# First batch's score stacks and row maxima into the last expert blocks, tables beside batch 0, layer-0 logits transposed

## The chip, the cores and the metric

The kernel runs on one core of one Trainium2 chip. The metric is device time in microseconds of one execution. The engines are TensorE (PE; its weight loads PEld), VectorE (DVE), ScalarE (ACT), GpSimd (POOL) and SyncE (SP, which here only issues DMAs). Each works through its own instructions in order and waits on semaphores.

## What is computed

Two transformer layers on 4 batches of 512 tokens with 256 channels, in float32. Each layer normalises, and adds an attention branch and a mixture of experts, both computed from the normalised rows. Cut to what matters here:

```python
x = hidden                                   # (4, 512, 256)
xn = layernorm(x)
q, k, v = rope(xn @ Wq.T), rope(xn @ Wk.T), xn @ Wv.T      # 16 heads of 16
attn = softmax(q k^T / 4) v
memory = (elu(k)+1)^T v                      # with its norm term, per head
combined = g * memory_readout(elu(q)+1) + (1-g) * attn
x = x + combined @ Wo.T + top2_experts(xn)   # 8 experts, 176 wide, router logits xn @ gate_w.T
xn = layernorm(x)
x = x + gated_linear_attention(xn, decay) + top2_experts(xn)   # 8 experts, 512 wide
```

## The kernel before

The program has three stages, with a barrier and freed semaphores between them (`end_stage`).

**Front (`layer0_front`).** It normalises, routes and runs layer 0's experts and projections. `front_order` writes the order of all engines by hand; each engine walks through it (`walk`) and takes the steps that it has a part in. First come the `prep` steps of the four batches: moments, normalising and turning, router logits (step 2), top two (step 3), weights (step 4). The logits are made per 128 tokens: 24 matmuls with 128 token columns as weights and 8 experts as moving columns, into psL. Then tokens are ranked by expert and gathered in 39 blocks of 128 rows (BLOCKS). A block is gate, turn_h, down, turn (gather and transpose of a later block); TensorE, ScalarE and VectorE pass it on in a chain, and GpSimd gathers and puts rows by indirect DMA. Between these items stand 39 `light` steps, ten per batch: projections of q and k (0, 2), rotation (1, 3), v (4), splitting into three bf16 parts (2 to 8), features, memory (8, 9), and at step 9 SP stores v, features and parts. They are given out evenly over the first 36 (BLOCKS - 3) blocks.

**Middle (`middle`).** Exact attention of layer 0 per batch and group of four heads, as softmax with row maxima. `qst` and `kst` are stacks of bf16 parts, loaded by `load` in 12 DMAs with one of values (`vst`) per group. `rows` makes scores for the maxima, `reduce` takes them on VectorE, `split_max` makes two bf16 parts, `turn_max` transposes them, and `send_max` on SP brings them through memory into two more rows of `qst`. So a group needs its maxima two groups ahead: before the loop, groups 0 and 1 of batch 0 are done in a prologue (L1654 to L1669 on VectorE, L1881 to L1888 on TensorE). In the loop, a group has four slots (`attend`): scores, exponentials, rows of the group after next, values. Beside batch 0 VectorE merges the expert rows of layer 0 that come back from memory (`merge`, two instructions a slot; four batches in four groups). SP loads these rows (L1210) after the stacks, constants and weights; they lie in `held`, with room for three batches. ScalarE makes tables and high parts of the weights before the loop (L1431 to L1442), GpSimd the low parts and the causal mask of the decays (L1345, L1348). Beside batches 1 to 3 run the projections of layer 1 for the batch before; they need the weights and tables.

**Layer 1 (`layer1_main`).** Its experts, with linear attention as light steps. It reads stacks per chunk, which lie in `held` too.

```python
order += [("turn", 0, 0), ("turn", 1, 0), ("gate", 0, 0), ("turn", 2, 0)]
rest, given, used = lights[1:], 0, 0
for b in range(BLOCKS + 1):
    for kind, n in (("gate", b + 1), ("turn_h", b), ("down", b - 1), ("turn", b + 3)):
```

Of the kernel before, what the change touches and what calls it, by code (L numbers as in the profile page):

```python
# [20 lines left out]
P = 128  # L21
# [193 lines left out]
F0H = F0 // 2  # L215
XSLOTS = 4
# [4 lines left out]
def front_order():  # L221
# [9 lines left out]
    for b in range(BLOCKS + 1):  # L231
        for kind, n in (("gate", b + 1), ("turn_h", b), ("down", b - 1), ("turn", b + 3)):
# [160 lines left out]
def layer0_front(nc, io, scratch, keep):  # L393


    with ExitStack() as ctx:
# [34 lines left out]
        hT = [[sb(f"hT{n}{i}", [F0H, 2, P], F32R) for i in range(2)] for n in range(2)]  # L431
        ymem = sb("y", [P, YSLOTS, D])
# [11 lines left out]

        ident_in, consts_in, x_in = sem("ident_in"), sem("consts_in"), sems("x_in", BATCHES)
# [4 lines left out]
        ones, xT_ps, xhi, xlo, logits_ps = (sem(n) for n in ("ones", "xT_ps", "xhi", "xlo", "logits_ps"))  # L450
# [48 lines left out]
        def _(sp):  # L499
# [44 lines left out]
            def light(n, s):  # L544
                if s == 9:
# [16 lines left out]
            walk({"prep": prep, "split": split, "light": light})  # L562
# [6 lines left out]
        def _(pool):  # L569
# [66 lines left out]

            nc.gpsimd.memset(neghalf[:, :], -0.5).then_inc(neghalf_set, 1)
            ranks.set_ones()
            pool.wait_ge(neghalf_set, 1)
            walk({"prep": prep, "split": split, "invert": invert, "turn": turn, "down": down, "light": light})  # L640

        @block.scalar
        def _(act):
# [95 lines left out]
        def _(dve):  # L739
# [109 lines left out]
            walk({"prep": prep, "rank": rank, "invert": invert, "turn": turn, "gate": gate, "turn_h": turn_h, "light": light})  # L849

        @block.tensor
        def _(pe):
            owner = {}

            def prep(n, s):
# [10 lines left out]
                elif s == 2:  # L866
                    pe.wait_ge(xlo, n + 1)
                    pe.wait_ge(routing.copied, n)
                    if n == 0:
                        pe.wait_ge(w_lo, WV + 1)  # L870
                    for t in range(TILES):
                        c = slice(t * P, (t + 1) * P)
                        mm = three(nc, psL[:, t * E:(t + 1) * E],
                                   [(xT[n][0][:, k, c], xT[n][1][:, k, c], wv[0][:, k, D:D + E], wv[1][:, k, D:D + E])
# [1587 lines left out]
```

## Time and profile before

| what | us |
|---|---|
| median of three runs (1073.11 to 1081.39) | 1075.36 |
| profiled execution, as a whole | 1074.24 |
| its span, first to last instruction | 1072.3 |
| front, to the last put of expert rows | 0 to 267 |
| middle's first instruction | 275.67 |

Times in the rows are microseconds from the start of the span unless marked ns. A timeline row gives start, duration, engine, line and operation, out and in, and how many alike were merged; in square brackets is the idle time of the engine before it and what ended that. L1453 is line 1453 of the kernel.

### The profile page before, as it was taken

The numbers are of one execution on the slowest core, as the hardware profiler recorded it, in microseconds if no ns is written. First come the engines' busy times: TensorE is split into PE (matmuls) and PEld (weight loads), VectorE is DVE, ScalarE is ACT, GpSimd is POOL, SyncE is SP. The second block draws the span as 40 slices with busy tenths as digits, with TensorE's granted clock in tenths as the row PEclk, the third lists the DMA queues.
The fourth block names the chain that finished last, engine by engine and source line by source line (L and its number), as shares of the span: only waits on it lengthen the run. The fifth ranks groups of instructions, "written<-read, shape, count | busy, mean of one in ns | idle before, by whom it ended". The sixth has DMA issues, their size and how long they took to land. (4 is left out here: it accounts for less than half of the span.)

```text
span 1072.3 us, 15783 instructions
## 1 busy us (share of the span) xinstructions
PE 866.9 (81%) x4924; PEld 551.0 (51%) x4924; DVE 586.2 (55%) x1296; ACT 423.6 (40%) x734; POOL 348.6 (33%) x265
## 2 busy tenths in 40 slices
PE   3825888787377889989999888657999999999991
PEld 3714877676011233444444345544666666666660
DVE  5595455453385987657766723393334434444435
ACT  2124564655043554774675574041222222222220
POOL 3175657567330000201110030043334344344321
PEclk9967799899556999999989988687999999999995
DMA  6321425334373222234233014449954533644317
GB/s 218 107 54 54 143 98 168 119 109 163 102 222 102 67 71 60 82 109 145 79 108 128 21 70 137 118 146 295 271 181 106 126 89 99 122 98 99 98 39 240
DMA packets 157346, 130.43 MB, mean 122 GB/s; under 512 B 63916, under 2 KB 138684, under 8 KB 157276
## 3 DMA queue, kind: packets, MB, share of 16 engines
q1 hardware_dynamic: 149788, 109.07, 34.5%
q0 software_dynamic: 7488, 20.46, 6.1%
q8 instruction: 40, 0.66, 0.3%
q14 instruction: 30, 0.25, 0.1%
HBM read 83.47 MB, written 46.01 MB: 121 GB/s over the span
## 5 line engine op out<-in xcount | busy, mean ns | idle before, releaser
L1453 DVE TENSOR_REDUCE b_negmax<-b_psM 128x1 f32<-128x512 f32 x256 | 162.8, 682 | 72.0 <-PE b_psM L1700 69.9
L1363 ACT ACTIVATE b_probs<-b_psE 128x512 f32<-128x512 f32 x256 | 138.8, 595 | 130.9 <-PE b_psE L1718 130.3
L1700 PE MATMUL b_psM<-b_kst,b_qst 96*128 96x512 bf16 x256 | 101.8, 443 | 37.5 <-DMA b_vst<-scratch_v 18.2
L1718 PE MATMUL b_psE<-b_qst,b_kst 98*128 98x512 bf16 x256 | 90.9, 419 | 20.9 <-ACT b_probs L1363 10.2
L2066 POOL DMA_INDIRECT scratch_ys<-d_y,put x39 | 39.6, 1016 | 129.3 <-ACT d_y L2098 127.9
L1718 PEld LDWEIGHTS b_psE<-b_qst,b_kst 98*128 98x128 bf16 x256 | 20.9, 99 | 112.0 <-ACT b_probs L1363 50.0
L2218 PE MATMUL d_psG<-d_w,d_xT 128*128 x156 | 76.6, 614 | 2.0 <-DVE d_xT L2117 1.6
L1727 PE MATMUL b_psV<-b_probs,b_vst 128*32 128x512 f32 x512 | 75.5, 664 | 3.0 <-ACT b_probs L1363 3.0
L1700 PEld LDWEIGHTS b_psM<-b_kst,b_qst 96*128 96x128 bf16 x256 | 24.6, 101 | 98.9 <-DVE b_negmax L1453 68.5
L2243 PE MATMUL d_psY<-d_w,d_hidden 128*128 x312 | 74.9, 383 | 0.0
L2226 PE MATMUL d_psU<-d_w,d_xT 128*128 x156 | 74.5, 600 | 0.0
L1305 POOL TENSOR_TENSOR b_combined<-b_both 128x256 f32<-128x256 f32 x16 | 11.6, 726 | 180.2 <-DVE b_both L1497 180.2
L2127 DVE TENSOR_TENSOR d_probs<-d_ps,decay 128x512 f32<-128x512 f32 x64 | 43.6, 687 | 46.7 <-PE d_ps L2261 46.6
L2072 POOL TENSOR_TENSOR d_rs<-d_ss,d_neghalf 128x16 f32<-128x16 f32 x16 | 46.9, 2929 | 56.8 <-DVE d_ss L2156 56.8
L2243 PEld LDWEIGHTS d_psY<-d_w,d_hidden 128*128 128x128 f32 x312 | 57.6, 190 | 12.9 <-issue 6.8
L2098 ACT ACTIVATE d_y<-d_psY 128x256 f32<-128x256 f32 x39 | 14.9, 383 | 122.1 <-PE d_psY L2243 122.1
L2122 DVE TENSOR_TENSOR d_hidden<-d_hidden,d_psU 128x512 f32<-128x512 f32 x39 | 26.8, 687 | 59.7 <-PE d_psU L2226 59.7
L608 POOL DMA_INDIRECT scratch_ys<-a_y,a_rk_put x39 | 43.2, 1108 | 43.8 <-ACT a_y L686 38.6
L2086 ACT ACTIVATE d_hidden<-d_psG 128x512 f32<-128x512 f32 x39 | 23.3, 597 | 86.0 <-PE d_psG L2218 86.0
L581 POOL DMA_INDIRECT a_xg<-scratch_xn,a_rk_take x39 | 41.3, 1059 | 27.9 <-issue 19.3
L2057 POOL DMA_INDIRECT d_xg<-scratch_xn,take x39 | 38.1, 977 | 21.4 <-issue 11.0
L2218 PEld LDWEIGHTS d_psG<-d_w,d_xT 128*128 128x128 f32 x156 | 27.3, 194 | 23.2 <-issue 23.1
(369 smaller groups left out, 1947.3 us busy)
## 6 DMA issues: line engine op xcount, KB each, us to landing
held<-scratch_parts SPq DMA_DIRECT2D x192, 64.0 KB, 3.1
scratch_parts<-a_part SPq DMA_DIRECT2D x12, 512.0 KB
b_qst<-scratch_parts SPq DMA_DIRECT2D x96, 64.0 KB, 2.2
b_kst<-scratch_parts SPq DMA_DIRECT2D x96, 64.0 KB, 2.2
scratch_parts<-b_part SPq DMA_DIRECT2D x24, 256.0 KB, 3.1
scratch_v<-a_v SPq DMA_DIRECT2D x4, 1024.0 KB, 4.5
b_vst<-scratch_v SPq DMA_DIRECT2D x16, 256.0 KB, 2.9
held<-scratch_ys SPq DMA_DIRECT2D x8, 512.0 KB, 6.8
```

What stands on the lines that cost most here:

```text
L581: nc.gpsimd.indirect_dma_start(xg[s], None, scratch["xn0"].rearrange("b s d -> (b s) d"), bass.IndirectOffsetOnAxis(ap=take[:, b:b + 1], a ...
L608: nc.gpsimd.indirect_dma_start(scratch["ys0"], bass.IndirectOffsetOnAxis(ap=put[:, b:b + 1], axis=0), y[b % YSLOTS], None).then_inc(put_ou ...
L1363: nc.scalar.activation(probs[k % PSLOTS][:, h, :], psE[h % 2][:, :], ACT.Exp, scale=float(HD) ** -0.5).then_inc(scores_used[h % 2], 1)
L1453: nc.vector.tensor_reduce(negmax[i][:, t, h:h + 1], psM[:, h % 2, :], AX_X, ALU.max, negate=True).then_inc(rows_used[h % 2], 1)
L1700: nc.tensor.matmul(psM[:, h % 2, :], qst[g][0:STACK, h, t * P:(t + 1) * P], kst[g][0:STACK, h, :], start=True, stop=True).then_inc(rows_re ...
L1718: nc.tensor.matmul(psE[h % 2][:, :], kst[g][0:STACKM, h, k * P:(k + 1) * P], qst[g][0:STACKM, h, :], start=True, stop=True).then_inc(score ...
L1727: mm = nc.tensor.matmul(psV[VW * h:VW * (h + 1), :], vst[g][:, k, VW * h:VW * (h + 1)], probs[k % PSLOTS][:, h, :], start=k == 0, stop=k = ...
L2072: nc.gpsimd.tensor_tensor(rs[:, :], ss[:, :], neghalf[:, :], ALU.pow).then_inc(rs_done, 1)
L2127: nc.vector.tensor_tensor(probs[g][:, :], (ps1 if g % 2 else ps0)[:, :], decay[:, HG * g:HG * g + HG, :].rearrange("p h c -> p (h c)"), AL ...
L2218: mm = nc.tensor.matmul(psG[:, :], xT[b % 2][:, k, :], weights(b, GATE + k * H1, H1), start=k == 0, stop=k == KT - 1)
L2226: mm = nc.tensor.matmul(psU[:, :], xT[b % 2][:, k, :], weights(b, UP + k * H1, H1), start=k == 0, stop=k == KT - 1)
L2243: mm = nc.tensor.matmul(psY[:, 0:D], hT[b % 2][:, k, :], weights(b, DOWN + k * D, D), start=k == 0, stop=k == HT1 - 1)
```

## The change

- `front_order`: light steps are spread over the first 29 blocks (AHEAD = BLOCKS - 10). Behind the turn item of blocks 29 to 32 stands a step `ones`, and behind each of the 32 items of blocks 30 to 37 a step `maxima`.
- The stacks of batch 0's four groups are loaded in the front, at light step 9 of batch n for group n, once that batch's parts are stored; values of all four after batch 3's. They lie on the memory of xT (stacks) and v32 (values), which now stays allocated through the middle; layer 1's chunks lie there as well, so their early load also waits for the last use of the values. Semaphores for stacks, values and maxima are kept across the stages (`Maxima`).
- A `maxima` step is one row-maximum matmul into psT and one reduction for groups 0 and 1; the splits come after steps 15 and 31, the transposes for group 0 after step 19, and SP sends group 0's maxima at step 20.
- `ones`: GpSimd fills the two rows of ones in `kst`.
- The middle has no prologue on TensorE and VectorE. SP issues identity, constants and weights, then returned rows of batches 0 and 1; batches 2 and 3 follow at slots 4 and 8, in a buffer of its own with room for two.
- ScalarE's tables and weight copies stand beside batch 0: sigmoid and small tables after slot 3, two decays after each of slots 4 to 11, weights after 12, 13 and 14. VectorE's waits for them move to the end of batch 0.
- Layer-0 logits: six matmuls with 8 expert columns as weights and 512 tokens moving, a ScalarE copy of 8x512 (step 2), and four transposes into psL (step 3).

```diff
+AHEAD = BLOCKS - 10
...
-            while given < min(len(rest) * used // (4 * (BLOCKS - 3)), len(rest)):
+            while given < min(len(rest) * used // (4 * AHEAD), len(rest)):
                 order.append(rest[given])
                 given += 1
+            if kind == "turn" and AHEAD <= b < AHEAD + GROUPS:
+                order.append(("ones", b - AHEAD, 0))
+            if 0 <= used - 1 - 4 * (AHEAD + 1) < 2 * 16:
+                order.append(("maxima", used - 1 - 4 * (AHEAD + 1), 0))
...
 # front, SP, light step 9
+                    sp.wait_ge(parts_stored, 48 * n + 48)
+                    sp.wait_ge(v_ps, n + 1)
+                    load_group(sp, scratch, keep, 0, n)
+                    if n == BATCHES - 1:
+                        sp.wait_ge(v_stored, 16 * BATCHES)
+                        sp.wait_ge(memory_ps, BATCHES)
+                        for g in range(GROUPS):
+                            load_values(sp, scratch, keep, 0, g)
+            def maxima(p, _):
+                if p == 20:
+                    sp.wait_ge(first.nmT_copied, 1)
+                    sp.dma_start(scratch["max"], nmT).then_inc(first.max_out, 16)
+                    sp.wait_ge(first.max_out, 16)
+                    sp.dma_start(qst[0][STACK:STACKM, :, :],
+                                 scratch["max"].rearrange("(a h) t -> a h t", a=2)).then_inc(first.max_in[0], 16)
...
 # front, GpSimd
+            def ones_rows(g, _):
+                pool.wait_ge(v_ps, g + 1)
+                pool.wait_ge(part_done[2], 2 * BATCHES)
...
+                nc.gpsimd.memset(kst[g][STACK:STACKM, :, :], 1.0).then_inc(ones_set, 1)
...
 # front, ScalarE, prep
+                elif s == 2:
+                    act.wait_ge(logitsT_ps, n + 1)
+                    act.wait_ge(logits_ps, n)
+                    nc.scalar.activation(logitsT[:, :], psH[0:E, :], ACT.Copy).then_inc(logitsT_done, 1)
...
 # front, VectorE
+            def maxima(p, _):
+                n, t, h = p // 16, p // HG % TILES, p % HG
+                if p == 0:
+                    dve.wait_ge(memory_ps, BATCHES)
+                    nc.vector.tensor_copy(identb, ident[:, :]).then_inc(identb_done, 1)
+                dve.wait_ge(first.rows_ready, p + 1)
+                nc.vector.tensor_reduce(first.negmax[n][:, t, h:h + 1], psT[:, h % 2, :], AX_X, ALU.max,
+                                        negate=True).then_inc(first.rows_used[h % 2], 1)
+                if p % 16 == 15:
+                    first.split_max(dve, n, n, False)
+                if p == 19:
+                    dve.wait_ge(first.nmT_ready, 1)
+                    nc.vector.tensor_copy(nmT, psT[0:2 * HG, 0, 0:SEQ // 2].bitcast(BF16)).then_inc(first.nmT_copied, 1)
...
 # front, TensorE
                     pe.wait_ge(xlo, n + 1)
-                    pe.wait_ge(routing.copied, n)
+                    pe.wait_ge(logitsT_done, n)
...
+                    three(nc, psH[0:E, :], [(wv[0][:, k, D:D + E], wv[1][:, k, D:D + E], xT[n][0][:, k, :], xT[n][1][:, k, :])
+                                            for k in range(KT)]).then_inc(logitsT_ps, 1)
+                elif s == 3:
+                    pe.wait_ge(logitsT_done, n + 1)
+                    pe.wait_ge(routing.copied, n)
                     for t in range(TILES):
...
+                        mm = nc.tensor.transpose(psL[:, t * E:(t + 1) * E], logitsT[:, t * P:(t + 1) * P], ident[0:E, 0:E])
...
+            def maxima(p, _):
+                n, t, h = p // 16, p // HG % TILES, p % HG
+                if p == 0:
+                    pe.wait_ge(memory_copied, KT * BATCHES)
+                if p % 16 == 0:
+                    pe.wait_ge(first.stack_in[n], 16 * GROUP_LOADS)
+                if p == 20:
+                    pe.wait_ge(first.nmT_copied, 1)
+                pe.wait_ge(first.rows_used[h % 2], 2 * (p // HG) + h // 2)
+                nc.tensor.matmul(psT[:, h % 2, :], qst[n][0:STACK, h, t * P:(t + 1) * P], kst[n][0:STACK, h, :],
+                                 start=True, stop=True).then_inc(first.rows_ready, 1)
+                if p == 19:
...
+                    for i in range(TILES):
+                        mm = nc.tensor.transpose(psT[0:2 * HG, 0, i * P // 2:(i + 1) * P // 2].bitcast(BF16),
+                                                 first.nmparts[0][:, i, :, :].rearrange("p a h -> p (a h)"), identb)
...
 # middle, SP
-            load(0, 0)
             sp.dma_start(ident[:, :], io["ident"]).then_inc(ident_in, 16)
-            load(0, 1)
...
-            load(0, 2)
-            send_max(1, 0, 0)
-            load(0, 3)
-            for n in range(BATCHES):
...
+            for n in range(2):
+                load_back(n)
+            def returns(k):
+                n = {4: 2, 8: 3}.get(k)
+                if n is not None:
+                    sp.wait_ge(merged, 2 * n - 2)
+                    load_back(n)
...
 # middle, early loads of layer 1 on SP
                 if alone(n):
+                    sp.wait_ge(probs_used, SLOTS * BATCHES)
...
 # middle, GpSimd
-            for g in range(GROUPS):
-                nc.gpsimd.memset(kst[g][STACK:STACKM, :, :], 1.0).then_inc(ones, 1)
...
 # middle, ScalarE
+            tasks = {3: (tables_small,), 12: (weights_hi(wqk, rqk),), 13: (weights_hi(wkv, rkv),), 14: (weights_hi(wr, rr),)}
+            tasks.update({4 + i: (tables_decay(i),) for i in range(HEADS // 2)})
...
 # middle, VectorE
-            for t in range(TILES):
-                reduce(0, 0, t)
-            split_max(0, 0, reused=False)
-            for t in range(TILES):
-                reduce(1, 1, t)
...
-            split_max(1, 1, reused=False)
...
             def ready():
                 dve.wait_ge(merged, 2 * BATCHES)
+                dve.wait_ge(g_done, 1)
...
+                dve.wait_ge(tables, TABLES)
+                dve.wait_ge(w_lo, 3)
...
 # middle, TensorE
+                        pe.wait_ge(value_in[g], 16 * b + 16)
...
-            for t in range(TILES):
-                rows(0, 0, t, 0, range(HG))
-            pe.wait_ge(identb_done, 1)
-            for t in range(TILES):
-                rows(1, 1, t, 0, range(HG))
-                if t == 0:
-                    turn_max(0, 0)
```

## Rows read from the trace of the kernel before

**Rows 1.** The page: busy time of engines, and the exponentials' group.
```profile
PE 866.9 (81%) x4924; PEld 551.0 (51%) x4924; DVE 586.2 (55%) x1296; ACT 423.6 (40%) x734; POOL 348.6 (33%) x265
...
L1363 ACT ACTIVATE b_probs<-b_psE 128x512 f32<-128x512 f32 x256 | 138.8, 595 | 130.9 <-PE b_psE L1718 130.3
```

**Rows 2.** Timeline from the end of the front to the middle's prologue.
```profile
267.05 0.97 POOL L608 DMA_INDIRECT scratch_ys<-a_y,a_rk_put  x1 [0.67 <-ACT a_y L686]
...
275.67 2.95 SPq L1173 DMA_DIRECT2D b_qst<-scratch_parts  x6
...
284.52 1.04 PE L1700 MATMUL b_psM<-b_kst,b_qst 96*128 96x512 bf16 x2 [18.16 <-DMA b_vst<-scratch_v]
...
285.17 11.04 DVE L1453 TENSOR_REDUCE b_negmax<-b_psM 128x1 f32<-128x512 f32 x16
```

**Rows 3.** Timeline from the prologue's second half to the start of group 1.
```profile
299.67 8.26 DVE L1453 TENSOR_REDUCE b_negmax<-b_psM 128x1 f32<-128x512 f32 x12
...
305.12 2.34 POOL L1345 TENSOR_TENSOR b_wkv<-b_outT,b_wkv 128x1024 fp32r<-128x1024 f32 x1
...
307.42 1.01 PE L1718 MATMUL b_psE<-b_qst,b_kst 98*128 98x512 bf16 x2 [0.22 <-issue]
...
307.67 4.50 POOL L1348 TENSOR_TENSOR decay<-decay,b_causal 128x2048 f32<-128x2048 f32 x1
308.03 4.17 DVE L1461 CAST b_nmparts<-b_negmax 128x16 bf16<-128x16 f32 x1
...
312.06 21.57 SPq L1210 DMA_DIRECT2D held<-scratch_ys  x8
...
319.32 0.88 DVE L1680 SCALAR_TENSOR_TENSOR xacc<-held,wts,xacc 128x256 f32<-128x256 f32 x2 [2.94 <-DMA held<-scratch_ys]
...
339.34 1.03 PE L1718 MATMUL b_psE<-b_qst,b_kst 98*128 98x512 bf16 x2 [6.89 <-DMA b_qst<-scratch_max]
```

**Rows 4.** Timeline of VectorE: ends of groups 1 and 3 of batch 0.
```profile
357.91 0.68 DVE L1483 COPY b_outT<-b_psV 128x512 f32<-128x512 f32 x1
...
387.55 0.68 DVE L1483 COPY b_outT<-b_psV 128x512 f32<-128x512 f32 x1
```

**Rows 5.** Windows in group 1: stretch, length, busy us of engines, PEclk, DMA, GB/s.
```profile
339.00:348.00 9.00, 8.66 (x27) 2.08 (x28) 4.98 (x9) 3.54 (x7) 0.00 (x0) 0.50 0.43 121
348.00:360.00 12.00, 10.59 (x51) 2.61 (x50) 10.89 (x22) 7.25 (x14) 0.00 (x0) 0.98 0.18 59
```

**Rows 6.** Timeline of ScalarE: copies of y that end blocks 0, 9, 27, 34, 36, 38.
```profile
95.58 0.38 ACT L686 ACTIVATE a_y<-a_psY 128x256 f32<-128x256 f32 x1 [0.43 <-PE a_psY L58]
...
140.10 0.38 ACT L686 ACTIVATE a_y<-a_psY 128x256 f32<-128x256 f32 x1 [0.34 <-PE a_psY L58]
...
225.22 0.38 ACT L686 ACTIVATE a_y<-a_psY 128x256 f32<-128x256 f32 x1 [0.34 <-PE a_psY L58]
...
258.91 0.38 ACT L686 ACTIVATE a_y<-a_psY 128x256 f32<-128x256 f32 x1 [0.33 <-PE a_psY L58]
...
262.97 0.38 ACT L686 ACTIVATE a_y<-a_psY 128x256 f32<-128x256 f32 x1 [0.33 <-PE a_psY L58]
...
266.39 0.38 ACT L686 ACTIVATE a_y<-a_psY 128x256 f32<-128x256 f32 x1 [1.25 <-PE a_psY L58]
```

**Rows 7.** VectorE: a reduction (ns min/median/max), and a block's instruction by lines.
```profile
L1453 DVE TENSOR_REDUCE b_negmax<-b_psM x256: 669/680/692, 285.2 to 610.9; 128x1 f32<-128x512 f32 x128
...
L790 DVE TENSOR_TENSOR a_xb<-a_psX,a_xb 128x256 fp32r<-128x256 f32 x13 | 5.5, 422 | 12.2 <-ACT a_xb L666 11.9
```

**Rows 8.** TensorE by lines, 95 to 267 us: busy, mean ns, idle before, releaser.
```profile
L964 PE MATMUL a_psT<-a_ident,a_rot 128*128 128x128 f32 x32 | 7.1, 395 | 17.6 <-DVE a_rot L830 17.6
```

**Rows 9.** Timeline of TensorE: batch 3's logits begin; then projections of 512 columns.
```profile
46.17 0.38 PE L56 MATMUL a_psL<-a_wv,a_xT 128*128 128x8 f32 x1 [2.37 <-DVE a_xT L769]
...
51.31 0.77 PE L56 MATMUL a_psT<-a_xT,a_wqk 128*128 128x512 f32 x1
...
55.62 0.39 PE L58 MATMUL a_psT<-a_xT,a_wqk 128*128 128x512 f32 x1
```

More of the change, by code:

```diff
@@ new lines, in front_order, with load_group @@
+    return order
+GROUP_LOADS = 2 * len(Q_PARTS)
+def load_group(sp, scratch, keep, b, g):
+    for op, dst, order in ((0, keep["qst"], Q_PARTS), (1, keep["kst"], K_PARTS)):
+        for i, part in enumerate(order):
+            row = (g % 2) * HG * HD
+            src = scratch["parts"][b, part, KT * op + g // 2, row:row + HG * HD, :]
+            sp.dma_start(dst[g][i * HD:(i + 1) * HD, :, :],
+                         src.rearrange("(h d) t -> d h t", d=HD)).then_inc(keep["first"].stack_in[g], 16)
@@ L639, in _ @@
             pool.wait_ge(neghalf_set, 1)
-            walk({"prep": prep, "split": split, "invert": invert, "turn": turn, "down": down, "light": light})
+            walk({"prep": prep, "split": split, "invert": invert, "turn": turn, "down": down, "light": light,
+                  "ones": ones_rows})
         @block.scalar
@@ L1429, in silu_v @@
                                      ACT.Silu).then_inc(v_done, 1)
-            act.wait_ge(consts_in, CONSTS)
-            nc.scalar.activation(gates[:, 1, :], gates[:, 1, :], ACT.Sigmoid).then_inc(g_done, 1)
-            for k in range(KT):
-                nc.scalar.activation(qdec[:, k, :], after[:, :], ACT.Exp, scale=ldrows[:, k:k + 1]).then_inc(tables, 1)
-            nc.scalar.activation(kdec[:, :], ldall[:, :], ACT.Exp, scale=before[:, 0:1]).then_inc(tables, 1)
-            nc.scalar.activation(cdec[:, :], ldrows[:, :], ACT.Exp, scale=float(CH)).then_inc(tables, 1)
@@ new lines, in tables_decay, with step, weights_hi @@
+            def tables_decay(i):
+                def step():
+                    for n in range(2 * i, 2 * i + 2):
+                        nc.scalar.activation(decay[:, n, :], rel[:, :], ACT.Exp, scale=ldall[:, n:n + 1]).then_inc(tables, 1)
+                return step
+            def weights_hi(dst, src):
+                def step():
+                    act.wait_ge(weights_in, WEIGHTS)
+                    act.wait_ge(padded, 3)
+                    nc.scalar.activation(dst[0][:, :, :], src[:, :, :], ACT.Copy).then_inc(w_hi, 1)
+                return step
@@ L2360, in two_layers, with early @@
             keep["mem"] = inner.enter_context(nc.sbuf_tensor("mem", [P, BATCHES * KT, MW], F32))
+            def early(name, shape, dt=F32):
+                return inner.enter_context(nc.sbuf_tensor(name, shape, dt))
+            keep["xT"] = [[early(f"xT{n}{i}", [P, KT, SEQ], F32R) for i in range(2)] for n in range(BATCHES)]
+            keep["v32"] = early("v32", [P, TILES, HEADS, VW])
+            keep["first"] = Maxima(nc, early)
+            stacks = [[t[:, :, :].rearrange("p a n -> p (a n)").bitcast(BF16) for t in pair] for pair in keep["xT"]]
+            keep["qst"], keep["kst"] = ([pair[i].rearrange("p (h n) -> p h n", h=HG) for pair in stacks] for i in range(2))
+            values = keep["v32"][:, :, :, :].rearrange("p t h w -> p (t h w)")
+            quarter = TILES * HG * VW
+            keep["vst"] = [values[:, g * quarter:(g + 1) * quarter].rearrange("p (t n) -> p t n", t=TILES) for g in range(GROUPS)]
             layer0_front(nc, io, scratch, keep)
```

169 lines of the change are left out of this document (85 added, 84 removed).

## The prediction, before the result was known

> **What bounds the kernel now.** I read the page first, then the timeline from the last expert block of layer 0 to the end of batch 0 of the middle stage, then the front stage by lines and by the copies that end its blocks. The page says TensorE is busy 81% of the span [rows 1]; the stretch that the change touches does not look like that. The last expert row is put out at 267.05. SP issues the first stack load of the middle at 275.67 (I call this point M), and TensorE gets its first row-maximum matmul at 284.52, after 18.16 us without work [rows 2]. Then VectorE paces a prologue of 32 reductions, 0.69 us each (16 in 11.04 us, 12 in 8.26 us) [rows 2, 3]. The first score comes only at 307.42, M+31.7. Group 0 is disturbed as well: a cast takes 4.17 us beside GpSimd's mask, the first merge waits 2.94 us for the returned expert rows, and group 1 waits 6.89 us for its row maxima, which SP could send only after the eight loads of returned rows that it had been issuing for 21.57 us [rows 3]. Group 1 starts at 339.34, M+63.7. After that two groups take 14.8 us each (outT copied at 357.91 and 387.55 [rows 4]), and there VectorE sets the pace: four reductions of 0.69 and two merges of 0.44 fill 3.6 of a slot's 3.7 us [rows 2, 3]. Batch 0 ends at 387.55, M+111.9.
>
> In the front stage the blocks end with a copy of y: 95.58 for the first, 266.39 for the last [rows 6]. From 258.91 to 262.97 lie two blocks with one light step that is not TensorE's, 2.0 us each, from there to 266.39 two with none, 1.7 each; I use 1.95 for a bare block. Nine blocks that carry one batch's light steps took 44.5 us (95.58 to 140.10), 42.6 (the next eighteen, halved) and 37.75 (225.22 to 262.97), so a batch of light steps adds some 20 to 27 us [rows 6].
>
> **The change part by part.**
>
> *Stacks, values and first maxima gone from the middle.* Twelve loads and one value load per group no longer stand ahead in SP's queue there, nor 32 matmuls on TensorE, 32 reductions and two splits on VectorE. Scores of group 0 can begin at M. The 52 loads move into SP's queue among the blocks, where it has only stores; they share the DMA engines with gathers that run four blocks ahead, and I price them at nothing, 2 us at most. What is late next: the first merge, in slot 0 on VectorE, ahead of the reductions of slot 1, for which TensorE's next row matmuls wait. It needs batch 0's returned rows. SP issues them after the identity, eight constants, the expert index and eight weights: 18 issues of 0.49 us (six in 2.95 us [rows 2]) are 8.8 us. In the profile they took 7.3 us from issue to the merge (312.06 to 319.32 [rows 3]), which I take again: M+16.1. Bounds: M+12, because the last two returned loads, issued by 333.63, and two small transfers behind them were through by 339.34 [rows 3], so that 3 us for two loads are possible; and M+20 if weights and four returned loads hinder each other. The maxima of group 1 go out behind the same loads, by about M+20, hidden behind group 0.
>
> From M+16.1: a merge (0.9), then three slots. TensorE will have idled and starts at 1.2 GHz: in group 1 the granted clock was 0.50 until 348 and 0.98 after it [rows 5], and that group took 18.6 us (339.34 to 357.91) in place of 14.8 [rows 3, 4]. So 11.1 for three slots plus 3.8, group 0 ends at M+31.9. Groups 1 to 3 at 14.8 each: M+76.3.
>
> *Tables, weight copies and mask beside batch 0.* ScalarE's 24 copies and tables lie in its idle time: a slot has four exponentials (256 in 138.8 us [rows 1], so 2.2 us of 3.7), and at most two tables or one copy go beside each; two table reloads round the sigmoid at the end of group 0 I put at 0.5 us, since VectorE and not ScalarE paces the slots (bounds 0 and 3). GpSimd's two subtractions of 2.34 us and the mask of 4.50 us [rows 3] now run beside slots 12 to 15. Before, the cast beside the mask took 4.17 us and ended with it, while reductions kept 0.69 us beside the subtractions [rows 3]. So merges and splits can be held, reductions can't. From their place I take 0.5 + 0.5 + 2.4 = 3.4 us; bounds 0 and 9.2 (all three whole). Batch 0 ends at M+80.2, against M+111.9: a gain of 31.7. With all bounds together it lies between 22 and 43.
>
> The Trainium skill (SBUF — State Buffer, Who interferes with whom) says that a VectorE instruction with two SBUF inputs, as a merge is, is shut out for the whole of a GpSimd instruction that reads SBUF, and that a reduction never is. Taken at its worst that is the 9.2 us, and the forecast below would be 6 us later.
>
> *Later loads of returned rows.* Batches 2 and 3 are loaded from slots 4 and 8, after merges 3 and 7. Behind that wait on SP stand the next stack loads, which have a group of slack. Merge 8 comes some 8 us after its issue, merge 12 about the same: nothing, by the 7.3 us above; a miss would cost up to 3 us each. Layer 1's early chunk loads now wait for the last values too, but SP reaches them after batch 3's attention anyway: nothing.
>
> *Maxima in blocks 30 to 37.* Four matmuls and four reductions per block, one behind each item. VectorE's own work per block is three instructions of at most 0.42 us, a reduction 0.68 [rows 7], 0.69 with its gap: 3 x 0.42 + 4 x 0.69 = 4.0 us per block in place of 1.95, over eight blocks 16.4 us; splits, identity cast, and the turn of the maxima at steps 19 and 20 (TensorE, VectorE and TensorE again in turn) 1.5: 17.9 us. TensorE needs less than a bare block's 1.95 and four times at most 0.39 [rows 9], 3.5 us, so VectorE sets it. Bounds: 14 (3.7 us, where successive instructions overlap by 0.1), and 30.7 with TensorE at half clock: twice 1.95 and four matmuls of 0.43, as two overlapping ones in 1.04 us [rows 2] allow, make 5.6 us per block. Queued behind the waits at steps 0, 16 and 20 is the block pipeline of TensorE, but the stacks were loaded long before. GpSimd's four fills of ones stand before puts with three buffers, and SP's waits for stored parts hold only loads that nobody needs yet: nothing.
>
> *Light steps in 29 blocks in place of 36.* The work is the same and blocks are only rearranged, but ten pairs of light steps share a block where there were three. TensorE already stands idle 17.6 us before the key turns, waiting for VectorE's features [rows 8]; with a bare block missing between two dependent steps, up to 1.95 us more can show. Nine new pairs are 17.6 us at most, zero at least. The three pairs of before sit in batches 1, 2 and 3, which were no slower than batch 0 without one (42.6, 42.6, 37.75 against 44.5 [rows 6]), so I lean to the low end: 6 us.
>
> *Logits transposed.* 24 matmuls took 5.14 us per batch (46.17 to 51.31); six of 512 columns cost 0.39 each (51.31 to 55.62 for eleven [rows 9]), 2.4 us, then a copy (0.6, by the 512-column exponentials' 595 ns [rows 1]), four transposes at the old logits' 0.21 each, 0.9, and handovers of 0.3: 4.2 us. But these transposes now stand behind the next batch's token transposes. Over four batches I take 2 us of gain, bounds 4 gained and 1 lost.
>
> **Sum.** -31.7 + 17.9 + 6 - 2 = -9.8 us. The profiled execution took 1074.24, of which 1072.3 is its span, so 1064.4; the median of the runs lies 1.1 above that execution: 1065.5. One per cent, about what a measurement of this kernel can tell from no change, is 10.75 us: below 1064.6 is faster, above 1086.1 slower. The forecast lies almost on the line.
>
> **Rivals.**
> *TensorE falls to 1.2 GHz in blocks 30 to 37.* It then waits for VectorE after every item, and all blocks pay 5.6 us in place of 4.0: 30.7 in place of 17.9, 1078.3, slower than before. It decides from a granted clock near 0.5 over most of these blocks; the break-even is 5.2 us per block. For it: the clock did fall in the middle where TensorE waited [rows 5]. Against it: TensorE would be busy four fifths of each block. The Trainium skill (TensorE: Matmul & The Clock Gate, A second HAM failure mode: psum-queue depth-cycling) tells of such a loss where TensorE idles briefly and often between groups of matmuls that cycle through PSUM banks, as these do; no row here shows it at that load.
>
> *Every pair of light steps costs a whole block.* 17.6 in place of 6: 1077, no change. For it: the idle time in [rows 8] is all chain. Against it: the earlier pairs cost nothing visible.
>
> *The returned rows don't hold.* They land near M+12, and pairs cost nothing: 4.1 + 6 less, 1055.4. For it: the last loads in [rows 3] were that fast. Against it: four loads and the weights go out together.
>
> *The change doesn't start group 0 earlier*, because group 0 only waits elsewhere: that is in the forecast with 16 of 31.7 us; it would have to wait to M+26 to undo the gain.
>
> **How the numbers follow.** Forecast 0.50 (its own range 1057 to 1073), half of it on either side of the line. Half clock 0.16, pairs 0.12, no hold 0.20, something unseen 0.02. Faster: 0.25 + 0.20 = 0.45. Slower: 0.05 of the half-clock case, with late merges and a full 9.2 us, and the unseen: 0.07. The rest, 0.48, is no change. The range reaches to the cases on both sides: 1050 to 1081.
>
> **What would show it.** First score within 2 us of the middle's first SP issue. First merge waiting for the returned rows to about M+16. Group 0's outT near M+32, then 14.8 us per group; one or two merges or casts of 2 us or more near slots 13 to 15. Y copies in blocks 30 to 37 about 4.0 us apart with the granted clock near 1.0. The light blocks over about 6 us later than bare reckoning gives; the middle starting 20 to 24 us later than 275.67. The prediction is wrong if the middle starts before 288 or after 305, or if batch 0 ends before M+70 or after M+90.

## The result, and the profile after

The change makes the kernel slower by half a per cent: median 1083.56 us over 20 runs against 1078.35 over 20 runs of the kernel before, made beside them, a ratio of 1.0052 (95% interval 1.0035 to 1.0069). I had forecast 1065.5 in a range of 1050 to 1081. The profiled execution took 1084.24 us, its span 1082.5. It lies 0.7 us above its median and the profiled one of before 4.1 below its own, so the two profiles are 10.0 us apart where the medians are 5.2. TensorE is as busy as before [rows 1]:

The page of the changed kernel, busy time of engines.
```profile
PE 866.4 (80%) x4868; PEld 546.1 (50%) x4868; DVE 584.5 (54%) x1297; ACT 427.8 (40%) x739; POOL 344.7 (32%) x265
```

The timeline around the start of the middle, answering to [rows 2, 3]:
```profile
293.48 0.97 POOL L679 DMA_INDIRECT scratch_ys<-a_y,a_rk_put  x1 [0.96 <-ACT a_y L769]
...
302.13 0.37 SPq L1302 DMA_DIRECT2D ident<-in_ident_dram  x1
302.31 1.01 PE L1825 MATMUL b_psE<-xT 98*128 98x512 bf16 x2 [9.52 <-PEq L72]
...
311.59 2.24 SPq L1288 DMA_DIRECT2D b_returned<-scratch_ys  x4
...
318.66 0.88 DVE L1781 SCALAR_TENSOR_TENSOR xacc<-b_returned,wts,xacc 128x256 f32<-128x256 f32 x2 [9.89 <-DMA b_returned<-scratch_ys]
...
329.88 1.28 ACT L1542 ACT_TABLE_LOAD   x1
...
331.40 1.28 ACT L1544 ACT_TABLE_LOAD   x1
331.50 0.68 DVE L1599 COPY b_outT<-b_psV 128x512 f32<-128x512 f32 x1
...
334.22 0.92 PE L1825 MATMUL b_psE<-xT 98*128 98x512 bf16 x2 [2.18 <-ACT b_probs L1472]
```

The middle (M, first issue on SP) starts at 302.13, 26.5 us later than before. The prologue is gone: the first score comes 0.2 us behind M, where it came 31.7 behind. The first merge waits for the returned rows to M+16.5. Batch 0 ends at 386.77 (below), M+84.6 against M+111.9 [rows 2, 4]: 27.2 us won, 26.5 paid in the front.

The copies of y that end blocks 0, 29, 37 and 38, answering to [rows 6]:
```profile
101.79 0.36 ACT L769 ACTIVATE a_y<-a_psY 128x256 f32<-128x256 f32 x1
...
256.29 0.38 ACT L769 ACTIVATE a_y<-a_psY 128x256 f32<-128x256 f32 x1 [0.55 <-PE a_psY L58]
...
290.90 0.38 ACT L769 ACTIVATE a_y<-a_psY 128x256 f32<-128x256 f32 x1 [0.33 <-PE a_psY L58]
292.82 0.38 ACT L769 ACTIVATE a_y<-a_psY 128x256 f32<-128x256 f32 x1 [1.54 <-PE a_psY L58]
```

Windows of groups 0 to 3 of batch 0 and of group 0 of batch 1, between the copies of outT (columns as in [rows 5]):
```profile
302.13:331.50 29.37, 19.09 (x71) 4.22 (x72) 14.01 (x29) 11.56 (x20) 1.24 (x4) 0.67 0.44 130
331.50:350.96 19.46, 16.23 (x70) 3.84 (x69) 14.36 (x29) 12.86 (x30) 0.00 (x0) 0.82 0.43 137
350.96:365.79 14.83, 13.37 (x70) 3.42 (x69) 14.19 (x30) 10.68 (x25) 0.00 (x0) 1.00 0.47 143
365.79:386.77 20.98, 14.60 (x68) 3.28 (x67) 20.61 (x30) 10.58 (x19) 9.53 (x4) 0.90 0.17 52
386.77:412.19 25.42, 24.14 (x122) 11.35 (x120) 16.52 (x33) 11.69 (x21) 2.86 (x4) 0.81 0.16 48
```

Three groups are longer than 14.8 us (batch 1's groups do more: its group 0 took 22.1 before). Group 1 begins with TensorE waiting 2.18 us behind two table loads on ScalarE (above); the granted clock, 1.00 from 325 to 333, is 0.50 from 335 to 341, which is 1.2 GHz. In group 3 the merges stand beside GpSimd:

Timeline of group 3, GpSimd, merges and TensorE's wait.
```profile
368.97 2.38 POOL L1454 TENSOR_TENSOR b_wqk<-b_rqk,b_wqk 128x1024 fp32r<-128x1024 f32 x1 [65.55 <-ACT b_wqk L1558]
...
369.31 2.72 DVE L1781 SCALAR_TENSOR_TENSOR xacc<-b_returned,wts,xacc 128x256 f32<-128x256 f32 x2
...
372.87 2.38 POOL L1454 TENSOR_TENSOR b_wkv<-b_rkv,b_wkv 128x1024 fp32r<-128x1024 f32 x1 [1.52 <-ACT b_wkv L1558]
...
374.35 1.58 DVE L1781 SCALAR_TENSOR_TENSOR xacc<-b_returned,wts,xacc 128x256 f32<-128x256 f32 x2
...
377.76 4.52 POOL L1457 TENSOR_TENSOR decay<-decay,b_causal 128x2048 f32<-128x2048 f32 x1
...
378.25 4.72 DVE L1781 SCALAR_TENSOR_TENSOR xacc<-b_returned,wts,xacc 128x256 f32<-128x256 f32 x2
...
383.62 1.21 PE L1806 MATMUL b_psM<-xT 96*128 96x512 bf16 x2 [3.32 <-DVE negmax L1579]
```

Each of the three pairs of merges ends 0.68 or 0.69 us after the GpSimd instruction (371.35, 375.25, 382.28), in place of 0.87 us after its own start: 1.85 + 0.71 + 3.85 = 6.4 us. Behind the last, TensorE has idled 3.32 us and its two matmuls take 1.21 us in place of 0.60; the next group has a granted clock of 0.81 (0.50 from 383 to 396) and takes 25.42 us in place of 22.09.

The table gives these stretches for all kernels run, in us: from the first gather to the last y, blocks 30 to 37 (between the copies of y of blocks 29 and 37; before and in logits_alone light steps stand in six of them), groups 0 to 3 of batch 0 from M, group 0 of batch 1, and from there to the end of batch 3's third group. The names of the experiments are those used below.

| kernel | gather to y | blocks 30-37 | g0 | g1 | g2 | g3 | b1 g0 | rest |
|---|---|---|---|---|---|---|---|---|
| before | 182.6 | 30.1 | 57.2 | 25.0 | 14.8 | 14.8 | 22.1 | 224.0 |
| changed | 208.3 | 34.6 | 29.4 | 19.5 | 14.8 | 21.0 | 25.4 | 230.3 |
| after_again | 209.9 | 34.5 | 29.7 | 19.6 | 14.8 | 21.0 | 26.9 | 227.0 |
| mask_pieces | 209.9 | 34.6 | 29.4 | 19.5 | 14.8 | 16.9 | 21.1 | 227.0 |
| sigmoid_early | 209.7 | 34.5 | 29.5 | 14.8 | 14.8 | 22.3 | 27.0 | 227.0 |
| returned_first | 210.0 | 34.7 | 19.1 | 19.5 | 14.8 | 21.0 | 25.4 | 230.3 |
| all_three | 210.2 | 34.6 | 22.9 | 14.8 | 14.8 | 16.9 | 21.1 | 224.0 |
| lights29 | 192.7 | 17.6 | 54.0 | 22.9 | 14.8 | 14.8 | 22.1 | 224.2 |
| logits_alone | 184.4 | 32.5 | 56.2 | 24.3 | 14.8 | 14.8 | 22.1 | 227.1 |
| maxima_narrow | 202.9 | 27.9 | 29.3 | 19.3 | 14.8 | 22.4 | 22.5 | 225.3 |
| steps_narrow | 202.4 | 27.3 | 30.1 | 18.0 | 14.8 | 22.3 | 25.7 | 226.0 |
| exp_gate | 209.6 | 34.6 | 19.1 | 15.0 | 14.8 | 16.9 | 21.1 | 226.6 |
| exp_gate_old_logits | 210.5 | 34.0 | 19.2 | 14.8 | 14.8 | 16.9 | 21.1 | 227.2 |

### The profile page after: what moved, and what is told of

Its sections match the earlier page's. It is cut to its first block and busy times, and to the rows that moved or that the text cites. A ratio compares the mean times of both kernels' runs of the same rounds, so it can differ in the third digit from the quotient of the medians.

```text
span 1082.5 us, 15716 instructions
## 1 busy us (share of the span) xinstructions
PE 866.4 (80%) x4868; PEld 546.1 (50%) x4868; DVE 584.5 (54%) x1297; ACT 427.8 (40%) x739; POOL 344.7 (32%) x265
## 5 line engine op out<-in xcount | busy, mean ns | idle before, releaser
L1579 DVE TENSOR_REDUCE negmax<-b_psM 128x1 f32<-128x512 f32 x224 | 142.0, 681 | 75.0 <-PE b_psM L1806 74.5
L1825 PE MATMUL b_psE<-xT 98*128 98x512 bf16 x256 | 90.9, 419 | 25.0 <-ACT b_probs L1472 12.1
L1806 PE MATMUL b_psM<-xT 96*128 96x512 bf16 x224 | 83.2, 421 | 26.0 <-DVE negmax L1579 22.8
L1825 PEld LDWEIGHTS b_psE<-xT 98*128 98x128 bf16 x256 | 21.0, 100 | 120.2 <-issue 62.0
L1835 PE MATMUL b_psV<-b_probs,v 128*32 128x512 f32 x512 | 78.6, 689 | 1.8 <-ACT b_probs L1472 1.8
L1806 PEld LDWEIGHTS b_psM<-xT 96*128 96x128 bf16 x224 | 21.2, 101 | 69.9 <-DVE negmax L1579 59.0
L879 DVE TENSOR_TENSOR a_h<-a_h,a_psG 128x176 f32<-128x176 f32 x39 | 13.1, 335 | 52.3 <-ACT a_h L756 52.3
```

Source lines behind the costliest of these rows:

```text
L1579: nc.vector.tensor_reduce(negmax[i][:, t, h:h + 1], psM[:, h % 2, :], AX_X, ALU.max, negate=True).then_inc(rows_used[h % 2], 1)
L1806: nc.tensor.matmul(psM[:, h % 2, :], qst[g][0:STACK, h, t * P:(t + 1) * P], kst[g][0:STACK, h, :], start=True, stop=True).then_inc(rows_re ...
L1825: nc.tensor.matmul(psE[h % 2][:, :], kst[g][0:STACKM, h, k * P:(k + 1) * P], qst[g][0:STACKM, h, :], start=True, stop=True).then_inc(score ...
L1835: mm = nc.tensor.matmul(psV[VW * h:VW * (h + 1), :], vst[g][:, k, VW * h:VW * (h + 1)], probs[k % PSLOTS][:, h, :], start=k == 0, stop=k = ...
```

## The experiments

### The changed kernel again (after_again)

> The changed kernel once more. Theory A (the slower groups of batches 1 to 3 follow from the change): the first group of batch 1 takes 25.4 us again where it took 22.1 before, and the other groups lose the same 6 us as in the first profile. Theory B (the clock falls at points that vary between executions): group 3 of batch 0 is again 21.0, but the later groups differ from the first profile by one to three us, up or down, with the granted clock. Time 1.005 of before by both.

1085.31 us (ratio to before 1.008, 1.0049 to 1.0112). Group 3 is 20.98 again, and group 0 of batch 1 is slow again, 26.9: that far theory A holds, though the size varies: in the kernels below that keep GpSimd's long instructions this group took 22.5 to 27.0 (22.5 in maxima_narrow, where the clock fell to 0.53 inside group 3 already). Behind it theory B does. The rest took 227.0, 3.3 less than in the first profile. The kernel logits_alone (below), whose middle is that of before, shows a step of the same size in code that nothing was done to.

### GpSimd's mask and subtractions in pieces (mask_pieces)

```diff
-            nc.gpsimd.tensor_tensor(decay[:, :, :], decay[:, :, :], causal[:, :].unsqueeze(1).to_broadcast((P, HEADS, CH)),
-                                    ALU.mult).then_inc(masked, 1)
+            for n in range(HEADS):
+                nc.gpsimd.tensor_tensor(decay[:, n, :], decay[:, n, :], causal[:, :], ALU.mult).then_inc(masked, 1)
```
and the subtractions of wqk and wkv in four column ranges each.

> GpSimd's mask in 16 instructions and its two large subtractions in 4 each, in the same places, with the same elements. Theory A (a merge is held until the GpSimd instruction that runs has ended): a merge is held by some 0.6 us at most, group 3 of batch 0 takes 15 to 16.5 us in place of 21.0, TensorE does not fall to 1.2 GHz there, the first group of batch 1 comes back from 25.4 to about 22, and the time falls by 6 to 9 us. Theory B (the two engines share the way to the memory, for so many elements): the pairs of merges lose the same 6.4 us in smaller portions, group 3 stays at 20 to 21, the time the same.

1074.42 us, 10.9 less than the changed kernel in the same comparison (some 7 by the ratio of 1.0052 in the result above), and level with before (0.9985, 0.9965 to 1.0005). Theory A, with group 3 at 16.9 a little above its range. Group 3, GpSimd and merges:
```profile
371.10 3.16 POOL L1456 TENSOR_TENSOR b_wqk<-b_rqk,b_wqk 128x256 fp32r<-128x256 f32 x4 [65.56 <-ACT b_wqk L1562]
371.44 1.55 DVE L1785 SCALAR_TENSOR_TENSOR xacc<-b_returned,wts,xacc 128x256 f32<-128x256 f32 x2
...
378.72 6.57 POOL L1462 TENSOR_TENSOR decay<-decay,b_causal 128x128 f32<-128x128 f32 x14
379.20 1.27 DVE L1785 SCALAR_TENSOR_TENSOR xacc<-b_returned,wts,xacc 128x256 f32<-128x256 f32 x2
```
Its windows, group 3 and group 0 of batch 1:
```profile
367.91:384.83 16.92, 14.15 (x71) 3.44 (x69) 16.78 (x29) 11.89 (x21) 12.69 (x22) 1.00 0.23 69
384.83:405.90 21.07, 19.23 (x118) 9.46 (x118) 16.59 (x35) 10.38 (x20) 4.15 (x8) 1.00 0.18 54
```
GpSimd now works longer (12.69 us in place of 9.53 in the group), but a pair of merges is held for 0.4 to 0.7 us. Against after_again, group 3 is 4.1 us shorter and the group behind it 5.8: the merges are held for less time, and TensorE keeps its full clock in both groups.

### Sigmoid earlier (sigmoid_early)

```diff
-            tasks = {3: (tables_small,), ...
+            tasks = {0: (tables_small,), ...
```

> Sigmoid and small tables after slot 0 in place of slot 3, while VectorE waits for the returned rows. Theory A (group 1 took 19.5 us because the two table loads stop TensorE at the group's start and leave it at 1.2 GHz): group 0 stays at 29 to 30 us, group 1 takes 15 to 16, the time falls by 3.5 to 5 us. Theory B (the clock falls there anyway, after the half-idle group 0): group 1 takes 17.5 to 19.5, the time falls by 2 or less.

1082.04 us, 3.3 less than the changed kernel. The intervals of the two overlap (1.0035 to 1.0073 of before here, 1.0049 to 1.0112 there), so the time by itself shows no gain. The trace does; the window of group 1:
```profile
333.39:348.21 14.82, 13.36 (x70) 3.40 (x69) 14.18 (x29) 10.66 (x25) 0.00 (x0) 1.00 0.59 179
```
Group 1 takes 14.82 us in place of 19.5, at a granted clock of 1.00: theory A. A part comes back later: group 3 takes 22.3 in place of 21.0.

### Returned rows of batch 0 first (returned_first)

```diff
             sp.dma_start(ident[:, :], io["ident"]).then_inc(ident_in, 16)
+            load_back(0)
...
-            for n in range(2):
-                load_back(n)
+            load_back(1)
```

> Returned rows of batch 0 loaded right behind the identity, ahead of constants and weights. Theory A (the first merge waits for nothing but its own rows): it comes 6 to 8 us after the middle's first SP issue in place of 16.5, group 0 ends 8 to 10 us earlier, and the time falls by 7 to 10 us. Theory B (the loads of weights and constants, or the maxima of group 1 that are sent behind them, then end last): the merge comes earlier, but group 1 waits at its start, and the time falls by 3 or less.

1074.51 us, 10.8 less (0.9983 of before, 0.9962 to 1.0003). The issue and the first merge, with the first scores of group 1:
```profile
304.25 0.37 SPq L1302 DMA_DIRECT2D ident<-in_ident_dram  x1
...
304.67 0.97 SPq L1288 DMA_DIRECT2D b_returned<-scratch_ys  x2
...
310.95 0.88 DVE L1781 SCALAR_TENSOR_TENSOR xacc<-b_returned,wts,xacc 128x256 f32<-128x256 f32 x2
...
324.58 0.61 PE L1825 MATMUL b_psE<-xT 98*128 98x512 bf16 x2 [1.67 <-DMA xT<-scratch_max]
```
The merge comes at M+6.7 and has no wait before it any more; group 0 takes 19.1 us in place of 29.7, a little more than theory A's 8 to 10. The wait of theory B is there, 1.67 us at the start of group 1, but that group takes 19.5 us with it as without.

### All three (all_three)

> The three edits together (mask and subtractions in pieces, sigmoid after slot 0, returned rows of batch 0 first). If the three losses are separate, batch 0 of the middle takes 84.6 less 5, 4 and 8, about 67 to 69 us from its first SP issue, the first group of batch 1 some 22, and the time is 18 to 22 us under the changed kernel, 1.2 to 1.6% under the kernel before. If they hide each other (the slots are then paced by VectorE at 1.2 GHz of TensorE), it is 8 to 14 under the changed kernel, at most 0.8% under the kernel before.

1064.10 us, 0.9865 of before (0.9836 to 0.9895); in the comparison with after_again the changed kernel stood at 1.008. Batch 0 takes 69.5 us from M. The three losses are separate (67 to 69 us were expected of batch 0), but for one thing: group 0 takes 22.9 us where it took 19.1 with the returned rows alone. The sigmoid now waits for its input in the first slots, and TensorE for the exponentials behind it:
```profile
314.59 0.22 ACT L1546 ACTIVATE b_gates<-b_gates 128x16 f32<-128x16 f32 x1 [2.66 <-DMA b_gates<-in_gate_attn_dram]
314.83 1.28 ACT L1548 ACT_TABLE_LOAD   x1
...
317.64 0.91 PE L1829 MATMUL b_psE<-xT 98*128 98x512 bf16 x2 [2.58 <-ACT b_probs L1476]
```

### Light steps in 29 blocks, alone (lights29)

```diff
-            while given < min(len(rest) * used // (4 * (BLOCKS - 3)), len(rest)):
+            while given < min(len(rest) * used // (4 * (BLOCKS - 10)), len(rest)):
```
This is the kernel before, with its own middle.

> The kernel before with one edit: light steps over 29 blocks in place of 36. Theory A (pairs of light steps in a block cost a part of a bare block): the last y copy comes 4 to 9 us later, the middle is the same, the time grows by 4 to 9 us. Theory B (the front only shifts the work): within 2 us.

1083.26 us, 1.0062 of before (1.0041 to 1.0084): by itself this one line loses as much as the whole change. The last copy of y comes 9.0 us later (275.34 against 266.39): theory A. From first gather to last y the edit adds 10.1 us (192.65 against 182.55), because the first gather, ahead of which nothing was edited, came 1.15 earlier. In its profile the middle is not the same as theory A has it: groups 0 and 1 with the prologue are 5.3 us shorter than before (77.0 against 82.2), and SP issued the eight loads of returned rows there in 18.17 us in place of 21.57; why was not taken apart. The stretch to 0.4 us behind the last y in both kernels, first before, then lights29:
```profile
83.84:266.77 182.93, 146.06 (x900) 134.35 (x900) 91.00 (x189) 101.59 (x205) 118.70 (x95) 0.88 0.37 124
```
```profile
82.69:275.72 193.03, 149.02 (x900) 136.51 (x900) 89.73 (x189) 101.64 (x205) 115.26 (x95) 0.87 0.35 118
```
The same 900 matmuls; TensorE idles 44.0 us in place of 36.9, and is busy 3 us longer. The bare blocks behind the light ones give a better price than I had (copies of y of blocks 29, 37, 38):
```profile
256.15 0.38 ACT L686 ACTIVATE a_y<-a_psY 128x256 f32<-128x256 f32 x1 [0.33 <-PE a_psY L58]
...
273.71 0.38 ACT L686 ACTIVATE a_y<-a_psY 128x256 f32<-128x256 f32 x1 [0.56 <-PE a_psY L58]
275.34 0.38 ACT L686 ACTIVATE a_y<-a_psY 128x256 f32<-128x256 f32 x1 [1.25 <-PE a_psY L58]
```
Eight take 17.56 us, 2.2 each, not 1.95. The maxima in the same blocks therefore add 34.6 - 17.6 = 17.0 us.

### Transposed logits, alone (logits_alone)

The kernel before with the hunks of the change that concern `logitsT` (front, TensorE and ScalarE, prep steps 2 and 3).

> The kernel before with the transposed logits alone. Theory A (what I forecast: 6 matmuls of 512 columns and 4 transposes for 24 matmuls): the first gather comes 1 to 3 us earlier. Theory B (the handovers over ScalarE eat the gain, as the profile of the changed kernel shows): the first gather comes 0 to 1 us later, and the time is the same within 1.5 us.

The first gather comes at 84.10 in place of 83.84: theory B, nothing is won. Nor can a loss be told: the first gather came between 82.7 and 85.3 in the three profiles with the old logits (before, lights29, exp_gate_old_logits), between 84.1 and 86.6 with the new. The time, 1.0022 (0.9999 to 1.0046), does not separate a small loss from none. The trace shows where the gain went: VectorE's low part of batch 3's rows (L769, L775) and its copy of batch 3's logits (L166), in the kernel before and then in this one:
```profile
44.90 1.22 DVE L769 TENSOR_TENSOR a_xT<-a_psG,a_xT 128x1024 fp32r<-128x1024 f32 x1 [0.93 <-ACT a_xT L652]
...
51.49 0.19 DVE L166 COPY a_rt_logits<-a_psL 128x32 f32<-128x32 f32 x1 [3.70 <-PE a_psL L58]
```
```profile
46.61 1.22 DVE L775 TENSOR_TENSOR a_xT<-a_psG,a_xT 128x1024 fp32r<-128x1024 f32 x1
...
51.74 0.19 DVE L166 COPY a_rt_logits<-a_psL 128x32 f32<-128x32 f32 x1 [3.36 <-PE a_psL L883]
```
Batch 3's logits take 1.5 us less, from their first matmul (46.17 before, 47.88 here) to the copy, but they begin 1.7 us later. Batch 2's logits, which now pass through ScalarE and are turned behind batch 3's token transposes, reach VectorE at 43.41 in place of 42.01, and VectorE takes batch 2's top two ahead of batch 3's low part. From 40 to 52 us TensorE was busy 6.8 us in place of 9.6, at a granted clock of 0.53 in place of 1.00. The profile also shows why a difference of 3 us in the time need not be the logits': group 3 of batch 1, where nothing was edited, in the kernel before and then in this one:
```profile
452.39:479.67 27.28, 25.11 (x136) 12.60 (x134) 15.27 (x30) 22.45 (x28) 2.13 (x1) 0.94 0.34 110
```
```profile
453.45:482.96 29.51, 26.97 (x137) 14.64 (x137) 15.27 (x30) 23.01 (x29) 2.15 (x1) 0.88 0.32 104
```
VectorE's busy time is the same to a hundredth; the granted clock is not.

### Narrow reductions, then narrow steps (maxima_narrow, steps_narrow)

```diff
-                nc.vector.tensor_reduce(first.negmax[n][:, t, h:h + 1], psT[:, h % 2, :], AX_X, ALU.max,
+                nc.vector.tensor_reduce(first.negmax[n][:, t, h:h + 1], psT[:, h % 2, 0:P], AX_X, ALU.max,
```

> The changed kernel with each of the 32 reductions in the blocks over 128 keys in place of 512 (so the maxima of groups 0 and 1 of batch 0 are over a quarter of the keys). A reduction falls from 0.68 to some 0.2 us. Theory A (VectorE's busy time paces blocks 30 to 37): 32 x 0.45, the eight blocks take some 14 us less, 18 in place of 32.4. Theory B (the chain TensorE, ScalarE, VectorE and back paces them, with a reduction in the way of each step and the matmuls added): 5 to 9 us less, 23 to 27.

The second kernel has the matmul over 128 keys as well:
```diff
-                nc.tensor.matmul(psT[:, h % 2, :], qst[n][0:STACK, h, t * P:(t + 1) * P], kst[n][0:STACK, h, :],
+                nc.tensor.matmul(psT[:, h % 2, 0:P], qst[n][0:STACK, h, t * P:(t + 1) * P], kst[n][0:STACK, h, 0:P],
```

> As the kernel with narrow reductions, and the 32 matmuls of the maxima are over 128 keys too. There the eight blocks took 27.9 us, against 34.5 with full reductions and 17.6 where no maxima stand in them. Theory A (the rest of 10.3 us is TensorE's time for 32 matmuls of 512 columns): a matmul falls by some 0.16 us, the blocks take 22 to 24 us. Theory B (the rest is the two handovers that each step puts into the chain): 26 to 28 us.

Reduction and matmul in blocks 30 to 37 of the changed kernel, the reduction of maxima_narrow, then both of steps_narrow (lines: busy us, mean ns, idle before):
```profile
L938 DVE TENSOR_REDUCE negmax<-a_psT 128x1 f32<-128x512 f32 x32 | 21.0, 679 | 0.3 <-PE a_psT L1096 0.3
...
L1096 PE MATMUL a_psT<-xT 96*128 96x512 bf16 x30 | 12.1, 404 | 2.8 <-DVE negmax L938 2.7
```
```profile
L938 DVE TENSOR_REDUCE negmax<-a_psT 128x1 f32<-128x128 f32 x31 | 8.8, 284 | 1.1
```
```profile
L938 DVE TENSOR_REDUCE negmax<-a_psT 128x1 f32<-128x128 f32 x31 | 8.0, 280 | 0.3
...
L1096 PE MATMUL a_psT<-xT 96*128 96x128 bf16 x30 | 6.8, 227 | 0.7 <-DVE negmax L938 0.6
```
The reductions' busy time falls by 12 us, the eight blocks by 6.6 (34.5 to 27.9; the 32.4 of the expectation was a shorter stretch). A matmul falls from 404 to 227 ns, and the blocks by only 0.6 more, to 27.3. So of the 17 us that the maxima cost, some 7 go with the width and 10 remain with quarter-wide steps, 0.3 us a step on average: theory B twice, by the time won. Of what the rest consists was not taken apart. The times are 1078.21 us for maxima_narrow (0.9999 of before, 0.9979 to 1.0018) and 1072.99 for steps_narrow (0.9969, 0.9948 to 0.9991).

Not all of the 7 us is width. The windows of the eight blocks in the changed kernel, of the one among them in which the maxima of group 0 are turned, and a VectorE line over the eight blocks:
```profile
256.67:291.28 34.61, 28.12 (x152) 20.22 (x150) 26.37 (x57) 10.66 (x30) 18.76 (x16) 0.95 0.33 103
274.37:281.14 6.77, 5.56 (x27) 4.03 (x25) 4.40 (x10) 1.47 (x5) 0.97 (x1) 0.75 0.07 22
```
```profile
L879 DVE TENSOR_TENSOR a_h<-a_h,a_psG 128x176 f32<-128x176 f32 x7 | 2.4, 337 | 7.5 <-ACT a_h L756 7.5
```
That block takes 6.77 us where the blocks ahead of it take some 4.4, at a granted clock of 0.75 (0.50 from 278 to 280); in both narrow kernels the clock is 1.00 throughout. This block and the next give 2.3 of the 6.6 us that maxima_narrow wins. VectorE is busy 26.4 of the 34.6 us and waits 7.5 for ScalarE's step behind the gate matmuls, so its sum alone does not pace the blocks at full width either.

### A version that beats both (exp_gate, exp_gate_old_logits)

All three edits, with the tables back behind slot 3 and the sigmoid as 1/(1+exp(-x)), which needs no other table:
```diff
-                nc.scalar.activation(gates[:, 1, :], gates[:, 1, :], ACT.Sigmoid).then_inc(g_done, 1)
+                nc.scalar.activation(gates[:, 1, :], gates[:, 1, :], ACT.Exp, scale=-1.0).then_inc(g_done, 1)
...
+                nc.vector.tensor_scalar(gates[:, 1, :], gates[:, 1, :], 1.0, None, ALU.add).then_inc(omg_done, 1)
+                dve.wait_ge(omg_done, 1)
+                nc.vector.reciprocal(gates[:, 1, :], gates[:, 1, :]).then_inc(omg_done, 1)
```

> As all three edits together, but the gate is made after slot 3 from an exponential on ScalarE and a reciprocal on VectorE, so no other table is loaded beside batch 0. Theory A (the 22.9 us of group 0 there, against 19.1 with the returned rows alone, are the table loads of slot 0): group 0 takes 19 to 20 us, groups 1 and 2 14.8 each, and the time is 3 to 5 us under that of all three, 1059 to 1061, 1.6% under the kernel before. Theory B (group 1 starts at 1.2 GHz whatever ScalarE does): group 0 19, group 1 18 to 19, the time that of all three.

> The same with the logits as in the kernel before. Theory A (the transposed logits cost something, 2.9 us with an interval from 0 to 5 where they stood alone): 1 to 4 us less than with them. Theory B (they cost nothing and that difference came from where the clock fell): the same within 1.5 us.

The second kernel also undoes the hunks of `logitsT`. exp_gate: 1060.86 us, 0.9846 of before (0.9818 to 0.9874). Groups 0 and 1 take 19.1 and 15.0: theory A for the groups; the time's interval overlaps that of all_three. With the old logits 1059.81, 0.9828 (0.9800 to 0.9856); the intervals overlap, so the logits stay open, and cost at most little. Batch 0 of the middle is now 65.8 us (303.73 to 369.58 in exp_gate), against 111.9 before.

## Why the prediction was wrong

The picture was right and the sum was not. The first score at M and the first merge at M+16.5 (forecast M+16.1) came as written, and no marker that I had set for "wrong" was passed (middle between 288 and 305, batch 0 ending between M+70 and M+90). Other signs failed: the middle began 26.5 us later and not 20 to 24, groups 1 and 3 took more than 14.8, and blocks 30 to 37 came 4.4 us apart, once 6.8, and not 4.0. Several terms were off, and all but the maxima against the forecast.

| term | forecast | measured | from |
|---|---|---|---|
| batch 0 of the middle | -31.7 | -27.2 | M+84.6 against M+111.9 |
| maxima in blocks 30 to 37 | +17.9 | +17.0 | 34.6 less the 17.6 of lights29 |
| light steps in 29 blocks | +6 | +10.1 | lights29; in the changed kernel 25.7 from first gather to last y, less 17.0 and 0.3 of the last block: 8.4, and 10.1 by the same sum in after_again |
| logits | -2 | +0.7 | first gather 84.53 against 83.84; +0.3 alone; both within its spread |
| group 0 of batch 1 | 0 | +3.3 | 25.42 against 22.09; +4.8 in after_again |

**The step that failed most** is that of the tables, weight copies and mask beside batch 0, 0.5 + 3.4 us there and nothing behind it. The mechanism was named, but I took less than half of the bound and ended its price at the end of batch 0. The merges lost 6.4 us and group 3 became 6.2 longer, and TensorE, held behind them, went into batch 1 at 1.2 GHz, 3.3 us more. Cutting the instructions gave back 9.9 us in these two groups. The rule of the Trainium skill (SBUF — State Buffer, Who interferes with whom) that I had weighed and not followed is what the trace shows, in that each held pair ended 0.68 or 0.69 us behind its GpSimd instruction, less than a pair's own 0.87. The sum of 9.2 us that I had from it was too high mainly because the merges began part of the way through.

**The table loads** that I put at 0.5 us, worked out from no row, because VectorE paces the slots, cost group 1 4.7 us (19.5 in place of 14.8). They stand at the start of a group, and TensorE's matmuls wait for the exponentials behind them. Group 0 gave back 2.5 of that (29.4 for 31.9).

**The light steps.** "The earlier pairs cost nothing visible" was read from nine- and eighteen-block averages; lights29 shows 9.0 to 10.1 us. The order has ten pairs where it had three, so seven more and not the nine that I counted: 1.3 to 1.4 us a pair, if it is all theirs. My rival with a whole block per pair gave 17.6, and would have given 13.7 with seven.

**The logits** got shorter as reckoned, but my proviso, that the transposes now stand behind the next batch's token transposes, and the way over ScalarE took all of it: the last batch's logits begin 1.7 us later and take 1.5 less.

**The maxima** came out right in part by luck. I added VectorE's busy time to 4.0 us per block, and blocks came 4.3 apart on average; but VectorE waited 7.5 of these 34.6 us for ScalarE, and a cut of 12 us of its busy time shortened the blocks by 6.6. The chain through the engines paces them too, and not VectorE's sum alone. The rival with TensorE at half clock came true in one block of the eight (0.75 over its 6.8 us); over all of them the granted clock was 0.95.

The measured terms add up to +3.9 us; the same stretches read directly give 26.5 later at M, 27.2 won in batch 0, 3.3 lost in batch 1: +2.5. The rest of the difference between the two profiles, 10.2 us by their spans, lies in later groups and layer 1 that the change hardly touches. They move by 3 us between executions of one kernel (230.3 and 227.0 in the changed kernel) and in logits_alone with the same middle as before (227.1 against 224.0). Whether the change makes the longer ones likelier was not settled; by medians the difference is 5.2.

## What to carry to other kernels

Work that fits an engine's idle time by its length can still hold another engine until it ends: price the hold by the instruction, and try a long GpSimd instruction in short ones where VectorE merges two tiles in SBUF beside it. Here a stall of TensorE of 3.3 to 3.7 us was paid again at half clock, by 0.4 to 4.9 us in the group behind it, so its price doesn't end with the wait. When work moves into a hand-ordered pipeline, count the handovers that each step adds and what is squeezed together to make room, and not only the busy time of the engine that does it.

## What the runs showed of the hardware

Cut into 25 instructions, GpSimd's work grew (3.16 us for four pieces of a subtraction that took 2.38 whole, 6.57 for 14 of the mask's 16 pieces where the whole took 4.52), and the kernel became 7 to 10.9 us faster. Behind the stall of 3.32 us the granted clock was 0.50 from 383 to 396 us, though TensorE was busy 12.1 of these 13 us. And a stretch of some 225 us took 230.3 and 227.0 us in two executions of the changed kernel, 224.0 and 227.1 in two kernels with the same middle, and the one group that was looked at in these two differs in the granted clock (0.94 and 0.88), with VectorE's busy time the same. The kernel before ran between 1070.0 and 1083.6 us over the comparisons, a spread wider than any single edit here.
